# Merging VectorE's passes of a state-space scan, its inputs one state ahead and its outputs one state behind, over two pairs of PSUM banks

## The chip, the cores and the metric

One core of a Trainium2 chip runs the kernel. The metric is device time in microseconds, the median of several runs. Engines are TensorE (PE; PEld is its weight load), VectorE (DVE), ScalarE (ACT), GpSimd (POOL) and SyncE (SP), which issues the DMAs. Everything is float32; PSUM has eight banks of 128 partitions x 512 float32.

## The reference, cut to what matters

Two layers, each an "attention" and a feed-forward part with a residual and a layer norm, on 4 sequences of 1024 tokens x 256 channels. The first is a gated recurrence (gate, below). The second is a selective state-space model with 16 states per channel, and this is the part that the change touches:

```
dA[t,d,n] = exp(dt[t,d] * A[d,n])
h[t,d,n]  = dA[t,d,n] * h[t-1,d,n] + dt[t,d] * x[t,d] * B[t,n]
y[t,d]    = sum over n of h[t,d,n] * C[t,n]
```

B and C are rows of a small projection of x: one value per token and state, the same for all channels.

## The kernel before, in words

**Chunks and steps.** The tokens are cut into 8 chunks of 512, two to a sequence. Channels lie on partitions, in two halves h = 0, 1 of 128, so one state of one chunk is two tiles of 128 x 512. A written-out pipeline works in steps; in each step five chunks are in work at five stages: *ahead* (load, convolution), *gate* (the gated recurrence, norm, first feed-forward up), *prep* (feed-forward down, in-projection, convolution, B, C and dt), *scan* (the 16 states) and *tail* (out-projection, second feed-forward, store). Each engine has its own `step` function, in which the calls stand in an order written by hand; each engine runs its list in that order, and semaphores tie them. Steps 3 to 7 have all or nearly all stages; scans run from 179 to 1036 us.

**One state n of a scan.** TensorE spreads row B(n) over all partitions into one bank (`spread_B`, one matmul of 97 x 512, L1188) and C(n) into another (`spread_C`). VectorE runs `state_input` (u * B, in two passes of 128 x 512, L876), `state_scan` (the recurrence, two scans of 128 x 512, L889) and `state_output` (h * C, two passes of 128 x 512, L902). ScalarE makes dA two tiles ahead or so (`state_decay`, L594), GpSimd adds hC into y (`sum_states`, L334, 128 x 1024) and in the first chunk of a sequence saves the last column (`save_carry`). The three banks `pBC` rotate over B and C: B(n) waits for the first scan of state n-1, C(n) for the second.

**Around it on VectorE.** Between the states stand the calls of the other stages: `add_ffn0`, `readout` (y * gate, L908, needs all 15 sums), `row_stats` and `row_moments` of the norms, `log_A`, `scaled_input`, `recurrence` (L832, two scans), `mconv_silu` (L852), `x_proj_low`, `dt_x` (L863).

**TensorE's list, in part.** down(0) last half, B(1), C(1), ..., `out_proj1` before B(3), two x2 transposes before B(4), `out_proj0` (16 matmuls, needs `recurrence`) before B(8), `x_proj` (needs `mconv_silu`) and a `down` of 16 matmuls before B(10), x1 transposes (need the norm of the gate stage) after B(12), eight `up` groups, then `down` groups of 16 matmuls with B(0) of the next chunk between them.

**GpSimd's and ScalarE's lists, in part.** GpSimd: `sum_states(1)`, then `row_scales` of the prep norm. ScalarE: `normalize` of prep, `gate_tanh(1,0)`, copy of x2's first transpose, `a_squared`, the second copy and `gate_tanh(1,1)`. At the end of a step: `step_sizes` (Softplus, makes dt), then the last two relus of the feed-forward, which the first `down` waits for.

**Banks.** `pA` (2) serves gate, up and x1 transposes, `pM` (1) x2 transposes, in-projection x, x_proj and dt, `pC` (2) the token-major results, `pBC` (3) B and C.

Of the kernel before, what the change touches and what calls it, by code (L numbers as in the profile page):

```python
# [1 line left out]

# [23 lines left out]
ACT = mybir.ActivationFunctionType  # L26
# [23 lines left out]
BRING = 3  # L50
# [11 lines left out]
NCHUNK = NSEQ * PER_SEQ  # L62
LAGS = LAG_AHEAD, LAG_GATE, LAG_PREP, LAG_SCAN, LAG_TAIL = -1, 0, 1, 2, 3


def build(nc, xT, x, par, ffb, rows, gateT, outT, inT, xpT, opT, w1a, w2a, w1b, w2b, out):
    ctx = ExitStack()
    with ctx:
# [85 lines left out]
        def C_bank(n):  # L154
            return pBC[(2 * n + 1) % BRING]

        def input_banks(n):

            return pBC[(2 * n - 1) % BRING], B_bank(n)

# [8 lines left out]
            B_mm C_mm dA_ready dBx_ready h_ready carry_saved hC_ready y_sum yg_ready eps_ready x3_seeded xtok_loaded passed  # L169
# [20 lines left out]
        def apart(eng):  # L190


            eng.sem_inc(S["passed"], 1)

        def num(ch):
            return PER_SEQ * ch[0] + ch[1]

        def first(ch):

            return isinstance(ch[0], int) and num(ch) == 0  # L200


        @block.sync
        def _(sp):
# [3 lines left out]

            def load(ch):
                q, p = ch  # L210
                c = num(ch)
                if not (isinstance(q, int) and c < 2):
                    sp.wait_ge(S["tap_ready"], H * PAD * (c - 1))
                sp.dma_start(xt[p][:], xT[:, :, bass.ds(q, 1), p * T:p * T + PAD + T].rearrange("k h o t -> k h (o t)")).then_inc(xt_loaded[p], 16)

            def load_rows(ch):
                q, p = ch
                if not first(ch):
                    sp.wait_ge(sum_ready[LN_GATE], num(ch))
                sp.dma_start(xtok[:], x[:, bass.ds(q, 1), p, :, :].rearrange("k o b d -> k (o b) d")).then_inc(S["xtok_loaded"], 16)  # L220
# [17 lines left out]
            def step(ahead, gate, prep, scan, tail):  # L238

                if ahead is not None:  # L240
                    load(ahead)
                    if first(ahead):
                        load_weights()
                if gate is not None:
                    load_rows(gate)
                if tail is not None:
                    q, p = tail
                    sp.wait_ge(norm_ready[LN_OUT], TB * (num(tail) + 1))
                    sp.dma_start(out[:, bass.ds(q, 1), p, :, :].rearrange("k o b d -> k (o b) d"), x3b[:]).then_inc(S["stored"], 16)
# [6 lines left out]
        def _(pool):  # L256
# [13 lines left out]
            def row_scales(n, ch):  # L270

                c = num(ch)
                pool.wait_ge(meanvar[n], TB * (c + 1))
                nc.gpsimd.tensor_tensor(ve[n][:], mv[n][:, :, 1], eps_rows[:, 0, :], ALU.add).then_inc(ve_ready[n], 1)  # L274
                nc.gpsimd.tensor_scalar(neg_mean[n][:], mv[n][:, :, 0], -1.0, None, ALU.mult).then_inc(neg_ready[n], 1)
                pool.wait_ge(ve_ready[n], c + 1)
                nc.gpsimd.tensor_tensor(rstd[n][:], ve[n][:], minus_half[:], ALU.pow).then_inc(rstd_ready[n], 1)  # L277
                pool.wait_ge(neg_ready[n], c + 1)
                pool.wait_ge(rstd_ready[n], c + 1)
                nc.gpsimd.tensor_tensor(shift[n][:], neg_mean[n][:], rstd[n][:], ALU.mult).then_inc(shift_ready[n], 1)  # L280

            def add_bias(n, layer, src, dst, done, ch):
                pool.wait_ge(norm_ready[n], TB * (num(ch) + 1))
                if n == LN_Y and not first(ch):
                    pool.wait_ge(S["stored"], 16 * num(ch))
                b2 = rows_sb[:, 1 + layer, :].unsqueeze(1).to_broadcast([P, TB, D])
                nc.gpsimd.tensor_tensor(dst[:], src[:], b2, ALU.add).then_inc(done, 1)

            def conv_add(ch, k):

                done = PAD * num(ch) + k - 1
                if k == 1:
                    pool.wait_ge(S["conv_first"], H * (num(ch) + 1))
# [3 lines left out]
                nc.gpsimd.tensor_tensor(conv[:], conv[:], tap[:], ALU.add).then_inc(S["conv_sum"], 1)  # L297

            def mconv_add(ch, k):

                done = PAD * num(ch) + k - 1
                if k == 1:
                    pool.wait_ge(S["mconv_first"], H * (num(ch) + 1))
# [3 lines left out]
                nc.gpsimd.tensor_tensor(cv[:], cv[:], v[:], ALU.add).then_inc(S["mconv_sum"], 1)  # L307

            def inv_rms(ch):
                c = num(ch)  # L310
                pool.wait_ge(S["sq_sum"], TB * (c + 1))
                nc.gpsimd.tensor_tensor(ms[:], ssq[:], eps_rows[:, 1, :], ALU.add).then_inc(S["ms_ready"], 1)
                pool.wait_ge(S["ms_ready"], c + 1)
                nc.gpsimd.tensor_tensor(rms[:], ms[:], minus_half[:], ALU.pow).then_inc(S["rms_ready"], 1)

            def rms_residual(ch):
                c = num(ch)
                pool.wait_ge(S["o_scaled"], TB * (c + 1))
                norm_w = rows_sb[:, 0, :].unsqueeze(1).to_broadcast([P, TB, D])
                nc.gpsimd.tensor_tensor(x1[:], x1[:], norm_w, ALU.mult).then_inc(S["o_weighed"], 1)  # L320
# [1084 lines left out]
```

## Time and profile before

| what | us |
|---|---|
| median of 3 runs (lowest, highest) | 1095.97 (1095.84, 1096.62) |
| the profiled execution: time, span | 1098.24, 1096.0 |
| VectorE busy in the span | 857.7 |
| TensorE busy in the span | 819.7 |
| ScalarE, GpSimd busy | 607.3, 581.6 |
| mean granted TensorE clock | 0.871 |

The span is first to last instruction. A duration in the profile runs from an instruction's start to its end, and two neighbours on an engine can overlap, so the distance between starts (the pitch) is what an instruction costs its engine.

### The profile page before, as it was taken

To read this page: it belongs to the slowest core of one execution; us is meant where nothing else is said; L and a number is where in the kernel's file an instruction comes from. 1 tells how busy PE (TensorE), PEld (TensorE's weight loads), DVE (VectorE), ACT (ScalarE), POOL (GpSimd) and SP (SyncE) were. 2 spreads that over 40 slices of the span, in tenths; PEclk is the share of its full clock that TensorE was granted. 3 is DMA by queue.
4 is the path that set the end of the run, shared out by engine and by line. 5 is a ranking of instruction groups with operands and counts; after the bars stand their busy time and mean duration, and the time that the engine had idled before them with its cause. 6 is when DMAs were issued, how large, how long until landed. Compare 5 with 4: busy or idle time off the path is not lost. (4 is left out here: it accounts for less than half of the span.)

```text
span 1096.0 us, 8799 instructions
## 1 busy us (share of the span) xinstructions
PE 819.7 (75%) x2536; PEld 500.2 (46%) x2536; DVE 857.7 (78%) x1226; ACT 607.3 (55%) x983; POOL 581.6 (53%) x419
## 2 busy tenths in 40 slices
PE   1358559736976997799869988899779889269376
PEld 0226226323643654465526563557346646145244
DVE  0302314999799999999999999998999899999811
ACT  3533545754666676667575767565853574534221
POOL 2041251567556864778285838683656474654410
PEclk9769769866988999899898998899889989569678
DMA  8000000000000010001000010001000000000000
GB/s 306 0 19 20 0 20 19 1 0 19 1 0 1 1 58 1 0 1 59 0 1 0 1 58 0 1 1 39 1 0 1 20 1 1 19 0 1 19 0 20
DMA packets 9215, 19.43 MB, mean 18 GB/s; under 512 B 1360, under 2 KB 3920, under 8 KB 9168
## 3 DMA queue, kind: packets, MB, share of 16 engines
q1 hardware_dynamic: 9168, 18.88, 5.0%
q8 instruction: 20, 0.33, 0.1%
q14 instruction: 27, 0.22, 0.1%
HBM read 14.68 MB, written 4.19 MB: 17 GB/s over the span
## 5 line engine op out<-in xcount | busy, mean ns | idle before, releaser
L334 POOL TENSOR_TENSOR y<-y,hC 128x1024 f32<-128x1024 f32 x112 | 285.7, 2551 | 57.4 <-DVE hC L902 54.1
L1075 PE MATMUL pC<-w,hT 128*128 128x256 f32 x1024 | 234.7, 384 | 16.1 <-ACT hT L532 16.0
L594 ACT ACTIVATE dA<-dt,A_neg 128x512 f32<-128x512 f32 x256 | 174.7, 719 | 122.4 <-DVE hs L889 122.2
L1188 PE MATMUL pBC<-stack,sel 97*128 97x512 f32 x256 | 158.1, 636 | 95.5 <-DVE hs L889 94.9
L1075 PEld LDWEIGHTS pC<-w,hT 128*128 128x128 f32 x1024 | 195.9, 192 | 52.9 <-issue 18.6
L876 DVE TENSOR_TENSOR pBC<-u,pBC 128x512 f32<-128x512 f32 x256 | 164.6, 687 | 43.6 <-PE pBC L1188 42.4
L902 DVE TENSOR_TENSOR hC<-hs,pBC 128x512 f32<-128x512 f32 x256 | 160.9, 669 | 1.5 <-PE pBC L1188 1.5
L889 DVE TENSOR_TENSOR_SCAN hs<-dA,carry,pBC 128x512 f32<-128x512 f32 x128 | 156.2, 1261 | 0.0
L889 DVE TENSOR_TENSOR_SCAN hs<-dA,pBC 128x512 f32<-128x512 f32 x128 | 148.5, 1200 | 0.0
L532 ACT ACTIVATE hT<-pA,ffb_sb 128x512 f32<-128x512 f32 x128 | 86.4, 687 | 101.6 <-PE pA L1068 101.4
L1188 PEld LDWEIGHTS pBC<-stack,sel 97*128 97x128 f32 x256 | 52.8, 206 | 163.4 <-DVE hs L889 138.9
L1068 PE MATMUL pA<-x1T,w 128*128 128x512 f32 x256 | 121.8, 624 | 1.4 <-ACT x1T L524 1.4
L1068 PE MATMUL pA<-tg,w 128*128 128x512 f32 x256 | 122.1, 613 | 0.7 <-ACT tg L524 0.7
L1075 PE MATMUL pC<-out_w,st 128*128 128x256 f32 x128 | 48.9, 565 | 57.4 <-DVE st L832 57.4
L510 ACT ACTIVATE x<-x,shift,rstd 128x256 f32<-128x256 f32 x96 | 49.8, 589 | 74.5 <-POOL shift L280 74.5
L297 POOL TENSOR_TENSOR conv<-conv,yg 128x1024 f32<-128x1024 f32 x24 | 58.0, 2418 | 55.4 <-ACT yg L453 55.4
L1068 PEld LDWEIGHTS pA<-x1T,w 128*128 128x128 f32 x256 | 51.3, 201 | 59.7 <-issue 57.5
L307 POOL TENSOR_TENSOR yg<-yg,v 128x1024 f32<-128x1024 f32 x24 | 59.9, 2497 | 33.7 <-ACT v L559 33.7
L1068 PEld LDWEIGHTS pA<-tg,w 128*128 128x128 f32 x256 | 51.0, 200 | 54.9 <-issue 51.5
L1068 PE MATMUL pA<-conv,gate_w 128*128 128x512 f32 x128 | 58.8, 606 | 22.1 <-POOL conv L297 22.1
L274 POOL TENSOR_TENSOR ve<-mv,eps_rows 128x4 f32<-128x4 f32 x32 | 6.5, 202 | 128.8 <-DVE mv L772 128.8
L342 POOL COPY carry<-hs 128x2 f32<-128x2 f32 x64 | 20.4, 319 | 97.2 <-DVE hs L889 97.2
(106 smaller groups left out, 1084.1 us busy)
## 6 DMA issues: line engine op xcount, KB each, us to landing
xt<-xT SPq DMA_DIRECT2D x8, 515.0 KB, 4.9
xtok<-x SPq DMA_DIRECT2D x8, 512.0 KB, 4.7
out<-x3b SPq DMA_DIRECT2D x8, 512.0 KB, 2.8
w<-w1a SPq DMA_DIRECT2D x1, 1024.0 KB, 9.5
w<-w2a SPq DMA_DIRECT2D x1, 1024.0 KB, 11.3
w<-w1b SPq DMA_DIRECT2D x1, 1024.0 KB, 8.2
w<-w2b SPq DMA_DIRECT2D x1, 1024.0 KB, 9.9
gate_w<-gateT SPq DMA_DIRECT2D x1, 512.0 KB, 7.5
```

Source lines behind the costliest of these rows:

```text
L297: nc.gpsimd.tensor_tensor(conv[:], conv[:], tap[:], ALU.add).then_inc(S["conv_sum"], 1)
L307: nc.gpsimd.tensor_tensor(cv[:], cv[:], v[:], ALU.add).then_inc(S["mconv_sum"], 1)
L334: nc.gpsimd.tensor_tensor(y[:], so_far, hC[:, n % CRING, :, :], ALU.add).then_inc(S["y_sum"], 1)
L510: nc.scalar.activation(rows[:, b, :], rows[:, b, :], ACT.Identity, bias=shift[n][:, b:b + 1], scale=rstd[n][:, b:b + 1]).then_inc(norm_rea ...
L532: nc.scalar.activation(hT[:, f, :], pA[f % 2][:], ACT.Relu, bias=ffb_sb[:, layer, f:f + 1]).then_inc(done, 1)
L594: nc.scalar.activation(dA[:, k % ARING, :], dt[:, h, :], ACT.Exp, scale=A_neg[:, h, n:n + 1]).then_inc(S["dA_ready"], 1)
L876: V.tensor_tensor(input_banks(n)[h][:], u[ch[1]][:, h, :], B_bank(n)[:], ALU.mult).then_inc(S["dBx_ready"], 1)
L889: V.tensor_tensor_scan(hs[:, n % HRING, h, :], dA[:, k % ARING, :], input_banks(n)[h][:], 0.0 if p == 0 else carry[:, n, h:h + 1], ALU.mul ...
L902: V.tensor_tensor(hC[:, n % CRING, h, :], hs[:, n % HRING, h, :], C_bank(n)[:], ALU.mult).then_inc(S["hC_ready"], 1)
L1068: mm = nc.tensor.matmul(dst, w[:, k, lo:lo + dst.shape[0]], src(k), start=k == 0, stop=k == H - 1)
L1075: mm = nc.tensor.matmul(dst[:, b * D:b * D + D], src(k, t0), w[:, k, :], start=k == 0, stop=k == nk - 1)
L1188: return nc.tensor.matmul(dst[:], sel[0:NXK, row:row + 1].to_broadcast([NXK, P]), stack[ch[1]][0:NXK, :], start=True, stop=True)
```

## The change

The four sets of roles are rearranged:

- `pM` is gone. A tensor `pS` of four banks holds two pairs; state n uses pair n mod 2. C(n) is spread into the bank of half 0, B(n) into that of half 1. x2 transposes, in-projection x, x_proj and dt use `pA`, with new waits.
- `state_input` and `state_output` are one pass of 128 x 1024 each, with B or C broadcast over the halves.
- On VectorE input(n+1) stands right behind the scans of state n, output(n) between the two scans of state n+1. What stood around the states stands now between input(n+1) and the scans of n+1. Output 15 and sum 15 run in the next step.
- B(n) waits for the second scan of state n-2, C(n) for the first scan of state n. TensorE calls C(n-1) where it called C(n); `dt_row` moves from before the second `down` of the tail to the end of the step.
- ScalarE: `gate_tanh(1,1)` stands before the second x2 copy, `step_sizes` behind the last relu.
- Chunks become objects with a length of their own, which stays 512; the `passed` increments go.

```diff
-        pM = bank("pM")
-        pBC = [bank(f"pBC{n}") for n in range(BRING)]
+        pS = ctx.enter_context(nc.psum_tensor("pS", [P, 2, H, T], F32))
+        def inputs(n):
+            return pS[:, n % 2, :, :]
+        def C_bank(n):
+            return pS[:, n % 2, 0, :]
         def B_bank(n):
-            return pBC[2 * n % BRING]
+            return pS[:, n % 2, 1, :]
...
             def state_input(ch, n):
-                for h in range(H):
-                    V.tensor_tensor(input_banks(n)[h][:], u[ch[1]][:, h, :], B_bank(n)[:], ALU.mult)...
+                if NS * c + n >= 2:
+                    dve.wait_ge(S["hC_ready"], NS * c + n - 1)
+                V.tensor_tensor(inputs(n)[:, :, 0:ch.T], u[ch.side][:, :, 0:ch.T],
+                                B_bank(n)[:, 0:ch.T].unsqueeze(1).to_broadcast([P, H, ch.T]), ALU.mult)...
...
             def state_output(ch, n):
+                dve.wait_ge(S["h_ready"], UNITS * c + H * n + H)
+                V.tensor_tensor(hC[:, n % CRING, :, 0:ch.T], hs[:, n % HRING, :, 0:ch.T],
+                                C_bank(n)[:, 0:ch.T].unsqueeze(1).to_broadcast([P, H, ch.T]), ALU.mult)...
...
             def spread_B(ch, n):
-                    pe.wait_ge(S["h_ready"], UNITS * c + H * (n - 1) + (1 if n else H))
+                if NS * c + n >= 2:
+                    pe.wait_ge(S["h_ready"], UNITS * c + H * (n - 1))
             def spread_C(ch, n):
-                    pe.wait_ge(S["h_ready"], UNITS * c + H * n)
+                pe.wait_ge(S["h_ready"], UNITS * ch.i + H * n + 1)
             def x2_transpose(ch, h, gate):
+                if gate is not None:
+                    pe.wait_ge(S["gate_tanh"], 4 * gate.i + h + 3)
             def x_proj(ch, tail):
+                if tail is not None:
+                    pe.wait_ge(S["relu1"], FB * tail.i + FB - 1)
             def dt_row(ch, gate):
+                if gate is not None:
+                    pe.wait_ge(S["relu0"], FB * gate.i + FB - 1)
...
             def step(ahead, gate, prep, scan, tail):      
+                    state_scan(scan, 1, 1)
+                    state_input(scan, 2)
+                    add_ffn0(prep, 1, tail)
+                    row_stats(LN_PREP, prep, x2[prep.side])
+                    readout(tail, gate)
+                    row_moments(LN_PREP, prep)
+                    state_scan(scan, 2, 0)
+                    state_output(scan, 1)
+                    state_scan(scan, 2, 1)
+                    state_input(scan, 3)
...
+                    scaled_input(gate)
+                    z_silu(prep, 1)
+                    recurrence(gate)
+                    state_scan(scan, 7, 0)
+                    state_output(scan, 6)
+                    state_scan(scan, 7, 1)
+                    state_input(scan, 8)
+                    state_scan(scan, 8, 0)
+                    state_output(scan, 7)
+                    state_scan(scan, 8, 1)
+                    state_input(scan, 9)
+                    mconv_silu(prep)
+                    state_scan(scan, 9, 0)
+                    state_output(scan, 8)
+                    state_scan(scan, 9, 1)
+                    state_input(scan, 10)
+                    x_proj_low(prep)
+                    row_stats(LN_GATE, gate, x1)
+                    state_scan(scan, 10, 0)
+                    state_output(scan, 9)
+                    state_scan(scan, 10, 1)
+                    state_input(scan, 11)
+                    row_moments(LN_GATE, gate)
```

## Rows read from the trace of the kernel before

**Rows 1.** The page's first part: each engine's busy time, share of the span, instructions.

```profile
PE 819.7 (75%) x2536; PEld 500.2 (46%) x2536; DVE 857.7 (78%) x1226; ACT 607.3 (55%) x983; POOL 581.6 (53%) x419
```

**Rows 2.** Waits of VectorE from 174 to 1037: total us, times, longest.

```profile
DVE pBC L876 <- PE pBC L1188: 42.4, 24, 4.0
```

**Rows 3.** Windows: stretch, its length, busy time per engine, granted TensorE clock, DMA.

```profile
576.06:582.13 6.07, 6.07 (x16) 4.93 (x17) 4.57 (x6) 0.84 (x4) 0.00 (x0) 0.54 0.00 0
590.63:593.90 3.27, 3.27 (x18) 2.88 (x16) 3.24 (x5) 3.27 (x6) 3.19 (x3) 1.00 0.00 0
509.90:515.00 5.10, 5.10 (x17) 4.21 (x17) 3.40 (x3) 5.07 (x9) 5.10 (x3) 0.67 0.27 95
522.99:637.93 114.94, 98.11 (x319) 60.94 (x318) 109.90 (x152) 74.53 (x122) 72.61 (x44) 0.93 0.04 14
```

**Rows 4.** The page's groups of instructions: the two passes that are merged.

```profile
L876 DVE TENSOR_TENSOR pBC<-u,pBC 128x512 f32<-128x512 f32 x256 | 164.6, 687 | 43.6 <-PE pBC L1188 42.4
L902 DVE TENSOR_TENSOR hC<-hs,pBC 128x512 f32<-128x512 f32 x256 | 160.9, 669 | 1.5 <-PE pBC L1188 1.5
```

**Rows 5.** Timeline of VectorE: start, length, line, tile, count, idle before and releaser.

```profile
522.99 1.29 DVE L876 TENSOR_TENSOR pBC<-u,pBC 128x512 f32<-128x512 f32 x2 [1.87 <-PE pBC L1188]
...
528.33 1.22 DVE L908 SCALAR_TENSOR_TENSOR yg<-y,zz 128x1024 f32<-128x1024 f32 x1
529.47 1.29 DVE L876 TENSOR_TENSOR pBC<-u,pBC 128x512 f32<-128x512 f32 x2
...
575.84 1.26 DVE L876 TENSOR_TENSOR pBC<-u,pBC 128x512 f32<-128x512 f32 x2
...
582.83 1.29 DVE L876 TENSOR_TENSOR pBC<-u,pBC 128x512 f32<-128x512 f32 x2 [2.20 <-PE pBC L1188]
...
587.57 1.22 DVE L852 SCALAR_TENSOR_TENSOR v<-v,yg 128x1024 f32<-128x1024 f32 x1
...
595.71 1.29 DVE L876 TENSOR_TENSOR pBC<-u,pBC 128x512 f32<-128x512 f32 x2
596.91 2.45 DVE L889 TENSOR_TENSOR_SCAN hs<-dA,carry,pBC 128x512 f32<-128x512 f32 x2
599.28 0.35 DVE L772 BATCH_NORM_AGGREGATE mv<-st 128x2 f32<-128x6 f32 x4
...
604.87 1.26 DVE L902 TENSOR_TENSOR hC<-hs,pBC 128x512 f32<-128x512 f32 x2
606.16 1.29 DVE L876 TENSOR_TENSOR pBC<-u,pBC 128x512 f32<-128x512 f32 x2
607.37 2.44 DVE L889 TENSOR_TENSOR_SCAN hs<-dA,carry,pBC 128x512 f32<-128x512 f32 x2
...
637.93 1.29 DVE L876 TENSOR_TENSOR pBC<-u,pBC 128x512 f32<-128x512 f32 x2 [0.73 <-PE pBC L1188]
```

**Rows 6.** Timeline of TensorE in the same step.

```profile
576.06 6.42 PE L1075 MATMUL pC<-out_w,st 128*128 128x256 f32 x16 [5.94 <-DVE st L832]
...
588.84 1.96 PE L1068 MATMUL pM<-v,xp_w 128*97 128x512 f32 x4 [0.27 <-DVE v L852]
...
593.90 0.81 PE L1188 MATMUL pBC<-stack,sel 97*128 97x512 f32 x2
...
604.17 1.04 PE L1086 MATMUL pA<-ident,x 128*128 128x128 f32 x8
...
626.52 3.69 PE L1075 MATMUL pC<-w,hT 128*128 128x256 f32 x16 [2.19 <-ACT hT L532]
```

**Rows 7.** Timeline of ScalarE in the same step.

```profile
536.53 2.08 ACT L510 ACTIVATE x<-x,shift,rstd 128x256 f32<-128x256 f32 x4
...
541.73 0.69 ACT L462 ACTIVATE tg<-pA,half_bias 128x512 f32<-128x512 f32 x1
```

**Rows 8.** Timeline of GpSimd in the same step.

```profile
529.63 2.37 POOL L334 TENSOR_TENSOR y<-hC 128x1024 f32<-128x1024 f32 x1 [11.64 <-DVE yg L908]
534.76 0.20 POOL L274 TENSOR_TENSOR ve<-mv,eps_rows 128x4 f32<-128x4 f32 x1 [2.77 <-DVE mv L772]
```

More of the change, by code:

```diff
@@ L184, in chunk @@
             def chunk(i):
-                return (i // PER_SEQ, i % PER_SEQ) if 0 <= i < NCHUNK else None
+                return CHUNKS[i] if 0 <= i < NCHUNK else None
             for i in range(LAG_AHEAD, NCHUNK + LAG_TAIL):
                 step(*(chunk(i - lag) for lag in LAGS))
[L190 to L200, printed above, removed]
         @block.sync
@@ L282, in add_bias @@
             def add_bias(n, layer, src, dst, done, ch):
[L283 to L287, printed above, removed]
+                pool.wait_ge(norm_ready[n], BLOCKS[ch.i + 1])
+                if n == LN_Y and ch.i > 0:
+                    pool.wait_ge(S["stored"], 16 * ch.i)
@@ L415, in step @@
                     conv_add(ahead, 3)
-                if scan is not None:
-                    sum_states(scan, 15)
             steps(pool, step)
@@ L933, in step @@
                 if scan is not None:
[L934 to L935 removed]
+                    state_scan(scan, 0, 0)
+                if tail is not None:
+                    state_output(tail, 15)
+                if scan is not None:
+                    state_scan(scan, 0, 1)
+                    state_input(scan, 1)
                 if prep is not None:
@@ L1139, in down @@
                 weight(ch, f"w2_{layer}")
-                pe.wait_ge(relu, FB * num(ch) + FB)
+                if layer == 0 and tail is not None:
+                    pe.wait_ge(sum_ready[LN_OUT], PAIRS[tail.i + 1])
+                if layer == 1 and gate is not None:
+                    pe.wait_ge(S["o_scaled"], BLOCKS[gate.i + 1])
+                elif layer == 1 and prep is not None:
+                    pe.wait_ge(S["zz_ready"], H * (prep.i + 1))
+                pe.wait_ge(relu, FB * ch.i + FB)
@@ L1349, in step @@
                 if scan is not None:
-                    spread_C(scan, 15)
+                    spread_C(scan, 14)
+                if prep is not None:
+                    dt_row(prep, gate)
                 if gate is not None:
-                    banks_for_down0(tail)
-                    down(0, gate, 0, 0)
+                    down(0, gate, 0, 0, tail=tail)
                 if prep is not None:
@@ L1357, in step @@
                     down(0, gate, 0, 1)
-                if prep is not None:
-                    spread_C(prep, 0)
+                if scan is not None:
+                    spread_C(scan, 15)
             steps(pe, step)
```

696 lines of the change are left out of this document (351 added, 345 removed).

## Prediction

> **What bounds the kernel now.** I read the engines' busy times first: VectorE 857.7 us and TensorE 819.7 us of a span of 1096.0 [rows 1]. Before the first scan at 179 us and after the last at 1036 us VectorE has little to do, so between them it is nearly full. Its waits there come next: 42.4 us before `state_input`, 24 times, for TensorE's spread of B [rows 2]. That is the first thing that the change could return. Then one full step, from the start of input(1) at 522.99 to the next at 637.93 [rows 5]: 114.94 us, of which TensorE is busy 98.1 at a granted clock of 0.93 [rows 3]. So TensorE has a sixth of the step free, and whoever moves VectorE's needs earlier against TensorE's list finds it late. The timelines say where they meet. VectorE idles 2.20 us before input(8) (TensorE is in `out_proj0`, which `recurrence` releases), and twice about 2 us where the steps join. TensorE idles before `out_proj0`, and from the x1 transposes at 604.17 to the `down` at 626.52 it works through [rows 5, 6].
>
> **The merge.** The rows give 687 and 669 ns for one pass [rows 4], two of each per state, but their spans overlap. What a pass costs is the pitch: from 606.16 to 607.37 is 1.21 us for both input passes, from 604.87 to 606.16 is 1.29 for both outputs, 0.1 of it latency because input(12) waits for the output just before (from 595.71 to 596.91, with no such wait behind it, is 1.20). The nearest row for 128 x 1024 without contention is `readout`: 528.33 to 529.47, 1.14 us [rows 5]. So a merge gives 0.06 on the input and about 0.04 on the output: 0.1 x 128 states = 13 us on VectorE. The 0.1 latency stays, now between input(n+1) and its first scan. Bounds: the merged pass reads a broadcast and writes PSUM, which no row shows in one pass; 1.14 (readout) below, 1.21 (as two) above, so 0 to 13 us. I take 1.14. VectorE's own work in that step falls from 110.1 (114.94 less 4.9 of stalls) to 108.5.
>
> The Trainium skill (VectorE: DVE Perf Modes, on the TRN2 errata) says that a large tile pays a fixed cost once which small tiles pay each; its formula for an fp32 add has 151 cycles, an estimate of 157 ns for each of 256 passes dropped, 40 us. The trace disagrees where passes follow each other: the pitch shows 0.04 to 0.06 us.
>
> **The waits of B.** B(n) may now run a state earlier. That helps where TensorE waited, and not where TensorE was late. But VectorE now wants B(n+1) ahead of output(n), and in three places something else between hardly shrinks. I follow the step of rows 5 to 8, with t = 0 at the start of input(1). VectorE's pieces: input 1.14, output 1.14, scan 1.2.
>
> *Out-projection.* Order is input(1), add_ffn0, scan, output(0), scan, input(2), add, stats, readout: it ends at t = 9.55. `out_proj1` takes 3.3 (as the 16 matmuls whose stretch is 3.27 [rows 3]), B(3) 0.6: ready at 13.65; VectorE wants it at 13.4. Stall 0.25.
>
> *The prep norm.* `row_moments` now stands before output(1), yet GpSimd's `sum_states(1)` stands before `row_scales`. Before, sum(1) began at 529.63, 5 us ahead of row_scales at 534.76 [rows 8]. Now output(1) ends at 12.2, sum(1) at 14.65 (2.37), and ScalarE's `normalize` begins 1.8 later (534.76 to 536.53 [rows 7, 8]), at 16.45. From there to gate_tanh(1,1) is 5.2 [rows 7]; with the first transpose behind gate_tanh(1,0) I take 5.35, so it ends at 22.45. The second transpose, which now needs that tanh's bank, and B(4) take 1.2: 23.65. VectorE wants B(4) at 21.85 (C(2) is late on the same path). Stall 1.8; before none.
>
> *Recurrence.* End of `recurrence` (575.84) to input(8) (582.83) is 7.0 with `out_proj0` between [rows 5, 6]. VectorE filled this with input, two scans and output (4.8); now input(7) is already done and it has 3.6. Stall 3.35 instead of 2.2. B(9), behind three up groups, is 0.45 late.
>
> *x_proj.* `x_proj` starts at 588.84, when `mconv_silu` ends; a `down` follows, B(10) starts at 593.90 [rows 5, 6]. With 0.6 for B: 5.7. Before, input(9) to x_proj_low and stats filled 6.9 (588.79 to 595.71). Now scan, output, scan: 3.55. Stall 2.15; before none.
>
> *Last stretch.* From the second scan of state 10 (599.28) TensorE sets the pace. x1's transposes came 4.9 later, 4.55 after row_moments [rows 5, 6]. Now input(11) stands before row_moments: 6.05 after the scan. TensorE then needs 22.35 to the first `down` (604.17 to 626.52), less 1.5 of the 2.19 that it waited for the last relu, which no longer stands behind Softplus, and 11.4 to input(1) (626.52 to 637.93). Sum 38.3; VectorE's own work there is 32.6: stall 5.7. ScalarE's dA for state 0, behind Softplus, a tap and a norm, comes within 0.2 of the same point.
>
> Stalls: 0.25 + 1.8 + 3.35 + 0.45 + 2.15 + 5.7 = 13.7, against 4.9. The step takes 108.5 + 13.7 = 122.2, 7.2 more. The same count gives +8 for the third step, +5.4 to +7 for the other full ones: 34 us over five. The first scan step (no tail) gets +3.8, mostly the prep norm. The last two get +5.5: x_proj +1.6 there, out_proj1 +2.5 in the last, where it runs at low clock and readout is moved to its front, the rest in output 15's move. Sum 43.
>
> **Clock.** After 5.94 us of idling TensorE's 16 matmuls of `out_proj0` took 6.07 us at granted clock 0.54 (near its lower level, 1.2 GHz), those of a `down` 3.27 at 1.00 (2.4 GHz), and one at 0.67 5.10 [rows 3, 6]. In the new order TensorE idles some 4 us before the x1 transposes, since it can run B(12) earlier but not them, right ahead of the stretch in which it sets the pace. A bound below is 0, above 2.8 per step (the two levels of rows 3); I take 1.5 in five steps, 8 us.
>
> The Trainium skill (TensorE: Matmul & The Clock Gate, part 1) says that idling gates the array to half rate until activity returns; the trace agrees at 576.06. By it the x1 stretch would start slow in every full step: 14 us for the 8, and 1153 in all.
>
> **Other parts.** Sum 15 and output 15 in the next step: `readout` wants y 8 us after input(1), sum 15 ends about 1 us after it, hidden. Dropping `passed` and the narrower slices of full length: nothing, they are no timed work. DMAs are the same. The `pA` waits of `up(1)` and gate_mm: their tiles are free some us before, hidden by the relu chain; if not, a few tenths. `dt_row` moves behind relu 6: dt is ready at 29.5 after the scan of state 10, wanted at 28.9, inside the stall counted. The lists of SP and GpSimd are moved past nothing, but for sum 15.
>
> Forecast: 1096.0 + 43 + 8 = 1147 us of span. The profiled run's time is 1098.24, the median of runs 1095.97, so the median is taken as the span.
>
> **Rivals.**
>
> (a) *VectorE is the bound and the waits go.* For it: TensorE has 16.8 us a step free, and B may run a state ahead. Then 42.4 + 13 go: 1041 us. It decides if TensorE is always a state ahead; against it stand `out_proj0` and `x_proj`, which hang on VectorE's results just before. A weaker form keeps those and loses only half the gain, 1070.
>
> (b) *Only the two fixed chains cost* (recurrence +1.15, x_proj +2.15 in six steps, +20), the rest is made good by relaxed waits and the merge (-10): 1106.
>
> (c) *TensorE slows further*: idling in three places a step, 2.8 us at each of two: +28 on the forecast's 43, 1167 or somewhat more.
>
> (d) *Merging saves the fixed cost in full*: two passes of 687 ns and two of 669 become two of 1216 to 1220 (readout's 1.22), so 0.28 us less busy in each of 128 states, 36 us, and all of it leaves the span: 1060. The overlap of neighbours in rows 5 speaks against it. The page on VectorE named above would have it so (an estimate of 40 us by its figure).
>
> **How the numbers follow.** Forecast and its near surroundings (1125 to 1165) 0.52; (b) 0.20; (c) 0.13; (a) 0.12; (d) 0.03. From 1100 to 1172 holds (b), the forecast and nearly all of (c): 0.8 or a little more. The forecast's own range is 1125 to 1165. A measurement of this kernel tells 0.2%, 2.2 us, from nothing. Faster: (a), (d) and a sliver of (b), 0.16; same 0.03; slower 0.81.
>
> **What would show it.** Rightness: busy VectorE falls by some 35 us (spans) while its waits before the merged input grow from 42 to about 100; in a full step waits of about 1.8 before input(4) or output(2), 3.3 before input(8), 2.1 before input(10), and a row of them from input(13) to input(1), TensorE without a gap there; x2's first transpose some 19 us after input(1) rather than 15.7; full steps of about 122. It is wrong if those waits are under 1 us, if input(10) is not held by x_proj's `down`, or if merged passes have a pitch far from 1.14.

## The result, and the profile after

| | before | after |
|---|---|---|
| median (lowest, highest), us | 1096.15 (1095.84, 1096.62) | 1154.88 (1152.17, 1158.47) |
| ratio to before, 95% interval | | 1.0537 (1.0501 to 1.0574) |
| profiled execution: time, span, us | 1098.24, 1096.0 | 1152.43, 1150.6 |
| mean granted TensorE clock | 0.871 | 0.857 |

Four runs of each. Those of the kernel after lie 6.3 us apart, so a difference to its median is known to some 3 us. The change costs 58.7 us on the medians, 54.6 on the spans of the two profiled executions.

The page's first part after, to be held against [rows 1]:

```profile
PE 828.8 (72%) x2536; PEld 509.5 (44%) x2536; DVE 839.4 (73%) x970; ACT 608.0 (53%) x983; POOL 558.2 (49%) x419
```

VectorE has 256 instructions fewer and is busy 18 us less, yet the span grew. The page's groups for the two merged passes [rows 4]:

```profile
L893 DVE TENSOR_TENSOR pS<-u,pS 128x1024 f32<-128x1024 f32 x128 | 155.7, 1217 | 90.5 <-PE pS L1220 90.0
L919 DVE TENSOR_TENSOR hC<-hs,pS 128x1024 f32<-128x1024 f32 x128 | 153.0, 1195 | 8.9 <-PE pS L1220 8.8
```

And VectorE's waits over the whole span (total, times, longest):

```profile
DVE pS L893 <- PE pS L1220: 90.0, 52, 5.4
...
DVE hs L908 <- ACT dA L609: 10.0, 11, 1.4
DVE hC L919 <- PE pS L1220: 8.8, 7, 3.6
```

The wait of `state_input` for TensorE's B went from 42.4 [rows 2] to 90.0 us, the wait of `state_output` for C from 1.5 [rows 4] to 8.8, and the scans wait for ScalarE's dA, which they did not before. I went from here to the steps. From input(1) of one chunk to input(1) of the next, in us (the eighth to the end of the last output):

| step | 1 | 2 | 3 | 4 | 5 | 6 | 7 | 8 |
|---|---|---|---|---|---|---|---|---|
| before | 110.4 | 113.8 | 112.5 | 114.9 | 113.6 | 115.0 | 89.8 | 80.1 |
| after | 114.1 | 120.9 | 122.2 | 122.4 | 123.3 | 122.4 | 98.4 | 82.7 |
| more | 3.7 | 7.2 | 9.7 | 7.5 | 9.7 | 7.4 | 8.6 | 2.6 |

So nothing single happened: every step pays. The eight sum to 56.4 us; outside them the kernel after is 1.8 us shorter. Over the eight, VectorE's waits (every idle stretch above 0.15 us) grew from 39.2 to 111.7 us. The rest of the stretch, counted from start to start, is VectorE's own work, and it fell from 810.4 to 793.6. Step 4, the one of [rows 5 to 8], now runs from 542.53 to 664.98. Its window, and two of its stretches:

```profile
542.53:664.98 122.45, 101.66 (x319) 63.18 (x318) 106.52 (x122) 74.67 (x122) 69.06 (x44) 0.90 0.04 13
611.47:614.18 2.71, 2.71 (x5) 1.00 (x6) 2.71 (x3) 0.00 (x0) 2.71 (x2) 0.65 0.00 0
631.36:637.00 5.64, 5.64 (x23) 4.76 (x24) 4.70 (x4) 4.49 (x8) 5.21 (x4) 0.70 0.01 3
```

VectorE's busy time fell from 109.9 [rows 3] to 106.5, TensorE's rose from 98.1 to 101.7 for the same 319 matmuls, at a granted clock of 0.90 instead of 0.93. VectorE's timeline, with the rows that begin and end the step and its main waits:

```profile
542.53 1.21 DVE L893 TENSOR_TENSOR pS<-u,pS 128x1024 f32<-128x1024 f32 x1
543.64 0.68 DVE L793 TENSOR_TENSOR x<-pC,x1b 128x512 f32<-128x512 f32 x1
...
556.09 1.23 DVE L893 TENSOR_TENSOR pS<-u,pS 128x1024 f32<-128x1024 f32 x1 [0.37 <-PE pS L1220]
...
562.45 1.22 DVE L919 TENSOR_TENSOR hC<-hs,pS 128x1024 f32<-128x1024 f32 x1 [0.52 <-PE pS L1220]
...
566.55 1.23 DVE L893 TENSOR_TENSOR pS<-u,pS 128x1024 f32<-128x1024 f32 x1 [1.69 <-PE pS L1220]
...
603.07 1.23 DVE L893 TENSOR_TENSOR pS<-u,pS 128x1024 f32<-128x1024 f32 x1 [3.63 <-PE pS L1220]
...
618.88 1.23 DVE L893 TENSOR_TENSOR pS<-u,pS 128x1024 f32<-128x1024 f32 x1 [4.06 <-PE pS L1220]
...
633.18 1.28 DVE L908 TENSOR_TENSOR_SCAN hs<-dA,carry,pS 128x512 f32<-128x512 f32 x1 [0.71 <-ACT dA L609]
...
638.14 1.23 DVE L893 TENSOR_TENSOR pS<-u,pS 128x1024 f32<-128x1024 f32 x1 [1.38 <-PE pS L1220]
...
661.54 1.22 DVE L908 TENSOR_TENSOR_SCAN hs<-dA,pS 128x512 f32<-128x512 f32 x1 [0.97 <-ACT dA L609]
...
664.98 1.23 DVE L893 TENSOR_TENSOR pS<-u,pS 128x1024 f32<-128x1024 f32 x1
```

The waits in brackets are of input(3), output(2), input(4), input(8), input(10), scan(12), input(13) and scan(0). With input(9) 0.71, input(14) 0.72, input(15) 0.63 and `dt_x` 0.23 they sum to 15.6 us. The merged input has a pitch of 1.11 us (542.53 to 543.64). TensorE's timeline says what each wait is for:

```profile
552.02 3.72 PE L1099 MATMUL pC<-op_w,yg 128*128 128x256 f32 x16 [2.08 <-DVE yg L926]
...
561.55 0.63 PE L1110 MATMUL pA<-ident,x 128*128 128x128 f32 x4 [2.13 <-ACT tg L477]
...
564.93 1.09 PE L1110 MATMUL pA<-ident,x 128*128 128x128 f32 x4 [2.52 <-ACT tg L477]
...
596.10 6.62 PE L1099 MATMUL pC<-out_w,st 128*128 128x256 f32 x16 [3.49 <-DVE st L849]
...
611.47 2.91 PE L1092 MATMUL pA<-v,xp_w 128*97 128x512 f32 x4 [2.66 <-DVE v L870]
614.18 4.37 PE L1099 MATMUL pC<-w,hT 128*128 128x256 f32 x16
...
631.36 1.07 PE L1110 MATMUL pA<-ident,x 128*128 128x128 f32 x8 [3.53 <-ACT x L525]
...
632.49 5.30 PE L1099 MATMUL pC<-w,hT 128*128 128x256 f32 x16
...
653.57 3.69 PE L1099 MATMUL pC<-w,hT 128*128 128x256 f32 x16 [0.41 <-ACT hT L547]
```

Six times TensorE stands still, for the readout, the prep norm and the tanh behind it (two transposes), the recurrence, the convolution and the gate's norm, with a spread that VectorE needs next *behind* the matmuls it stands at. Against [rows 6], `x_proj` takes 2.91 instead of 1.96, and two groups of 16 matmuls 4.37 and 5.30 where 3.62 is usual. That is the lower clock: 0.65 and 0.70 in the two short windows above, and 0.81 from 614.18 to 618.19, where the 4.37 us lie. GpSimd's timeline shows the start of the norm's chain, `sum_states(1)` ahead of the row scales [rows 8]:

```profile
554.67 2.36 POOL L350 TENSOR_TENSOR y<-hC 128x1024 f32<-128x1024 f32 x1 [10.80 <-DVE hC L919]
556.99 0.20 POOL L290 TENSOR_TENSOR ve<-mv,eps_rows 128x4 f32<-128x4 f32 x1
```

### The profile page after: what moved, and what is told of

Same layout as the page of the kernel before. It is cut to its first block and busy times, and to the rows that moved or that the text cites. A ratio compares the mean times of both kernels' runs of the same rounds, so it can differ in the third digit from the quotient of the medians.

```text
span 1150.6 us, 8402 instructions
## 1 busy us (share of the span) xinstructions
PE 828.8 (72%) x2536; PEld 509.5 (44%) x2536; DVE 839.4 (73%) x970; ACT 608.0 (53%) x983; POOL 558.2 (49%) x419
## 3 DMA queue, kind: packets, MB, share of 16 engines
HBM read 14.68 MB, written 4.19 MB: 16 GB/s over the span
## 5 line engine op out<-in xcount | busy, mean ns | idle before, releaser
L350 POOL TENSOR_TENSOR y<-y,hC 128x1024 f32<-128x1024 f32 x112 | 264.2, 2359 | 184.0 <-DVE hC L919 181.5
L1099 PE MATMUL pC<-w,hT 128*128 128x256 f32 x1024 | 242.2, 392 | 4.8 <-ACT hT L547 4.8
L609 ACT ACTIVATE dA<-dt,A_neg 128x512 f32<-128x512 f32 x256 | 174.0, 718 | 120.9 <-DVE hs L908 120.8
L893 DVE TENSOR_TENSOR pS<-u,pS 128x1024 f32<-128x1024 f32 x128 | 155.7, 1217 | 90.5 <-PE pS L1220 90.0
L1220 PE MATMUL pS<-stack,sel 97*128 97x512 f32 x256 | 153.8, 630 | 79.3 <-DVE hs L908 79.2
L908 DVE TENSOR_TENSOR_SCAN hs<-dA,carry,pS 128x512 f32<-128x512 f32 x128 | 162.6, 1270 | 6.3 <-ACT dA L609 4.2
L908 DVE TENSOR_TENSOR_SCAN hs<-dA,pS 128x512 f32<-128x512 f32 x128 | 154.8, 1210 | 8.5 <-ACT dA L609 5.8
L919 DVE TENSOR_TENSOR hC<-hs,pS 128x1024 f32<-128x1024 f32 x128 | 153.0, 1195 | 8.9 <-PE pS L1220 8.8
L547 ACT ACTIVATE hT<-pA,ffb_sb 128x512 f32<-128x512 f32 x128 | 86.7, 684 | 108.3 <-PE pA L1092 108.2
L1220 PEld LDWEIGHTS pS<-stack,sel 97*128 97x128 f32 x256 | 52.7, 209 | 129.2 <-DVE hs L908 106.7
L1110 PE MATMUL pA<-ident,x 128*128 128x128 f32 x128 | 27.4, 368 | 84.9 <-ACT x L525 48.7
L1099 PEld LDWEIGHTS pC<-out_w,st 128*128 128x128 f32 x128 | 36.2, 291 | 67.9 <-issue 60.0
```

The lines of the kernel that those rows point to most:

```text
L350: nc.gpsimd.tensor_tensor(y[:, :, 0:ch.T], so_far, hC[:, n % CRING, :, 0:ch.T], ALU.add).then_inc(S["y_sum"], 1)
L547: nc.scalar.activation(hT[:, f, 0:ch.T], pA[f % 2][:, 0:ch.T], ACT.Relu, bias=ffb_sb[:, layer, f:f + 1]).then_inc(done, 1)
L609: nc.scalar.activation(dA[:, k % ARING, 0:ch.T], dt[:, h, 0:ch.T], ACT.Exp, scale=A_neg[:, h, n:n + 1]).then_inc(S["dA_ready"], 1)
L893: V.tensor_tensor(inputs(n)[:, :, 0:ch.T], u[ch.side][:, :, 0:ch.T], B_bank(n)[:, 0:ch.T].unsqueeze(1).to_broadcast([P, H, ch.T]), ALU.mul ...
L908: V.tensor_tensor_scan(hs[:, n % HRING, h, 0:ch.T], dA[:, k % ARING, 0:ch.T], inputs(n)[:, h, 0:ch.T], 0.0 if ch.opens else carry[:, n, h: ...
L919: V.tensor_tensor(hC[:, n % CRING, :, 0:ch.T], hs[:, n % HRING, :, 0:ch.T], C_bank(n)[:, 0:ch.T].unsqueeze(1).to_broadcast([P, H, ch.T]), ...
```

## The experiments

Theory: VectorE now asks for B a state earlier, and TensorE's list, which kept its order, has it behind fixed chains. Then moving the calls in the lists gives the time back and the merge is innocent. Rivals: the merged passes themselves cost; VectorE's work bounds the step and a removed wait comes back as the next; the clock of TensorE is the main loss. Before ran beside each group of kernels, at medians of 1096.06 to 1096.94 us. Ratios are to it, with 95% intervals; "less" and "more" are to the median of the kernel after, unless another is named.

**The merge undone, the order kept.**

```diff
-                V.tensor_tensor(inputs(n)[:, :, 0:ch.T], u[ch.side][:, :, 0:ch.T],
-                                B_bank(n)[:, 0:ch.T].unsqueeze(1).to_broadcast([P, H, ch.T]), ALU.mult)...
+                for h in range(H):
+                    V.tensor_tensor(inputs(n)[:, h, 0:ch.T], u[ch.side][:, h, 0:ch.T], B_bank(n)[:, 0:ch.T], ALU.mult)...
...
-                V.tensor_tensor(hC[:, n % CRING, :, 0:ch.T], hs[:, n % HRING, :, 0:ch.T],
-                                C_bank(n)[:, 0:ch.T].unsqueeze(1).to_broadcast([P, H, ch.T]), ALU.mult)...
+                for h in range(H):
+                    V.tensor_tensor(hC[:, n % CRING, h, 0:ch.T], hs[:, n % HRING, h, 0:ch.T], C_bank(n)[:, 0:ch.T], ALU.mult)...
```

> The changed kernel with each merged pass taken apart again into two passes of 128 x 512, at the same places and in the same banks; nothing else. By the theory of the order (time is lost where VectorE asks for B and C before the work that stands ahead of them on TensorE can be done) this is a little slower: pitch 1.20 and 1.18 us instead of 1.12 and 1.11, 0.15 us x 128 = 19 us on VectorE, of which most lies in stretches where it waits for TensorE anyway (the waits of a full step are 15 of 122 us, and the last stretch is TensorE's), so +6 to +14 over the 1154.9. By the rival (the merged pass over two banks, with a broadcast operand, is what costs) it returns a good part of the 59 us: under 1130.

Measured: 1158.03 us, 1.0556 (1.0541 to 1.0572). That is 3.2 us more than after, where 6 to 14 were expected, with intervals that overlap: in the new order the merge costs no time and brings at most a few us. VectorE's own work over the eight steps, counted as above, is 804.6 us against 793.6, so 11.0 more, but its waits are 104.7 against 111.7. The merge does save work on VectorE, and two thirds of it went into waits. The timeline of VectorE shows a state with nothing between, the input's two passes at 1.18:

```profile
1064.59 1.26 DVE L894 TENSOR_TENSOR pS<-u,pS 128x512 f32<-128x512 f32 x2
1065.77 1.27 DVE L908 TENSOR_TENSOR_SCAN hs<-dA,carry,pS 128x512 f32<-128x512 f32 x1
...
1069.33 1.26 DVE L894 TENSOR_TENSOR pS<-u,pS 128x512 f32<-128x512 f32 x2
```

And the kernel after, the same part of the last chunk:

```profile
1059.49 1.21 DVE L893 TENSOR_TENSOR pS<-u,pS 128x1024 f32<-128x1024 f32 x1
1060.78 1.28 DVE L908 TENSOR_TENSOR_SCAN hs<-dA,carry,pS 128x512 f32<-128x512 f32 x1
...
1064.28 1.21 DVE L893 TENSOR_TENSOR pS<-u,pS 128x1024 f32<-128x1024 f32 x1
```

Split, the state takes 4.74 us. Merged, it takes 4.79: the scan starts 1.29 behind the input, not 1.11, because it now needs the whole merged input just ahead of it. Where a call stands between them, this 0.18 is hidden: from 1064.28 to the next input at 1069.49 is 5.21 with a 0.60 us addition in it, 4.61 without; split, the same state takes 4.73 (1069.33 to 1074.66, less 0.60).

**Only the output merged, in the kernel before.** No order is changed; output(n) stands where it stood.

```diff
-                for h in range(H):
-                    dve.wait_ge(S["h_ready"], UNITS * c + H * n + h + 1)
-                    V.tensor_tensor(hC[:, n % CRING, h, :], hs[:, n % HRING, h, :], C_bank(n)[:], ALU.mult)...
+                dve.wait_ge(S["h_ready"], UNITS * c + H * n + H)
+                V.tensor_tensor(hC[:, n % CRING, :, :], hs[:, n % HRING, :, :],
+                                C_bank(n)[:].unsqueeze(1).to_broadcast([P, H, T]), ALU.mult)...
```

> The kernel before with only state_output merged into one pass of 128 x 1024 with C broadcast over the halves; the order, the three banks and the input passes stay. By the pitch (1.11 us for the merged output in the changed kernel, 1.18 for two in the kernel before) 0.07 us x 128 = 9 us less on VectorE, about a third of it lost where it waits for TensorE: 1087 to 1092. By the rule of a fixed cost for each pass dropped it would be 128 x 0.16 = 20 us less, 1076. If merging costs by itself it is above 1096.

Measured: 1116.08 us, 1.0171 (1.0148 to 1.0195), 19 more than before beside it. A miss in the sign. VectorE's timeline:

```profile
611.11 1.28 DVE L876 TENSOR_TENSOR pBC<-u,pBC 128x512 f32<-128x512 f32 x2
612.30 2.44 DVE L889 TENSOR_TENSOR_SCAN hs<-dA,carry,pBC 128x512 f32<-128x512 f32 x2
614.88 1.22 DVE L901 TENSOR_TENSOR hC<-hs,pBC 128x1024 f32<-128x1024 f32 x1
616.13 1.29 DVE L876 TENSOR_TENSOR pBC<-u,pBC 128x512 f32<-128x512 f32 x2
```

And the same state in before, whose output and next input stand in [rows 5]:

```profile
601.32 1.28 DVE L876 TENSOR_TENSOR pBC<-u,pBC 128x512 f32<-128x512 f32 x2
602.51 2.44 DVE L889 TENSOR_TENSOR_SCAN hs<-dA,carry,pBC 128x512 f32<-128x512 f32 x2
```

From the start of the scans to the output it is 2.58 us (612.30 to 614.88); in before it is 2.36 (602.51 to 604.87), since there the output's first pass needs only the first scan. From output to input it is 1.25 instead of 1.29. So 0.04 is gained, as in the prediction, and 0.22 lost, and the state takes 5.02 us instead of 4.84. Over the eight steps the scans cost 22.7 us more from start to start and the outputs 6.0 less: 16.7 of the 19. VectorE's other instructions took 4.7 more (`mconv_silu` alone 6.2), and its waits 3.1 less. The merged output alone loses; what lets it pay is the order of the change, which puts a scan of the next state between.

**B(10) ahead of x_proj.** The change's TensorE list, with one call moved.

```diff
+                    spread_B(scan, 10)
                     x_proj(prep, tail)
                     ...
-                    spread_B(scan, 10)
```

> The changed kernel with one call moved on TensorE: the spread of B(10) stands ahead of x_proj and the down of 16 matmuls instead of behind them. By the theory of the order the wait before input(10) (4.06 us in the full step of 542 to 665) falls to under 0.5 in each of the six steps that have it, and the time by 18 to 24 us, to 1131 to 1137. By the rival of load (TensorE has too much work at too low a clock, so a wait relieved comes back at the next B or C) the time falls by less than 8 us, and the waits before output(9), input(11) or input(13) grow by what input(10) loses.

Measured: 1122.50 us, 1.0228 (1.0210 to 1.0246): 32.4 less than after, where 18 to 24 were expected; the rival of load is out. In step 4 (116.1 us) input(10) no longer waits, and input(11) waits 0.54. Its TensorE:

```profile
597.92 1.26 PE L1220 MATMUL pS<-stack,sel 97*128 97x512 f32 x3
601.62 3.31 PE L1092 MATMUL pA<-v,xp_w 128*97 128x512 f32 x4 [2.44 <-DVE v L870]
604.76 3.62 PE L1099 MATMUL pC<-w,hT 128*128 128x256 f32 x16
```

`x_proj` is still slow, but nobody waits behind it. What exceeds the theory is clock: the 16 matmuls of `out_proj0` took 5.24 us instead of 6.62, which cut input(8)'s wait from 3.63 to 2.25, and the `down` behind the x1 transposes took 3.62 instead of 5.30, which took away input(13)'s 1.38.

**C(2) and B(4) ahead of the transposes of x2.**

```diff
+                    spread_C(scan, 2)
                     x2_transpose(prep, 0, gate)
-                    spread_C(scan, 2)
+                    spread_B(scan, 4)
                     x2_transpose(prep, 1, gate)
-                    spread_B(scan, 4)
```

> The changed kernel (1154.9) with two TensorE calls moved: C(2) ahead of x2's first transpose, B(4) ahead of its second. By the theory of the order the waits before output(2) and input(4) of 0.5 and 1.7 us go in six steps or seven, 12 to 16 us: 1139 to 1143. By the rival of load less than 5 us, as the wait turns up at the next C.

Measured: 1136.18 us, 1.0363 (1.0348 to 1.0379), 18.7 less, somewhat more than the 12 to 16 expected. The waits of output(2) and input(4) are gone from the full step (a new one of 0.84 at input(5)).

**B(8) and C(7) ahead of out_proj of half 0.**

```diff
+                    spread_B(scan, 8)
                     out_proj0(gate, prep)
-                    spread_B(scan, 8)
+                    spread_C(scan, 7)
...
-                    spread_C(scan, 7)
...
+                    spread_B(scan, 9)
...
-                    spread_B(scan, 9)
```

> The kernel after, with TensorE's spread B(8) moved ahead of out_proj of half 0, C(7) right behind it, and B(9) moved behind the fifth of the up-projection's tiles of the second half. Nothing else is moved. Theory of order (a fixed chain in TensorE's own queue makes input(8) and input(9) late): in a full step of the kernel after, input(8) waited 3.63 us and input(9) 0.71; of these 4.3 us some 3 to 4 go, out_proj moves behind the input, and x_proj and B(10) follow no earlier than their own chain allows. Six steps by 3 to 4 us: 18 to 24 us less, 1131 to 1137 us. Rival (VectorE's time is only moved to the next wait, input(10), whose 4.1 us is set by the convolution behind the recurrence and TensorE's clock): under 6 us less, 1149 to 1155.

Measured: 1125.38 us, 1.0259 (1.0244 to 1.0274): 29.5 less, more than the theory asked for, and far from the rival. A full step fell from 122.4 to 117.4: the 4.3 of input(8) and (9) are gone, input(13)'s 1.38 too, input(10) waits 3.28 instead of 4.06, and new are 1.19 at output(7) and 0.89 at scan(9). In its TensorE the later stretches run faster too:

```profile
601.17 1.96 PE L1092 MATMUL pA<-v,xp_w 128*97 128x512 f32 x4 [1.07 <-ACT hT L547]
...
619.40 1.07 PE L1110 MATMUL pA<-ident,x 128*128 128x128 f32 x8 [3.53 <-ACT x L525]
...
620.54 3.62 PE L1099 MATMUL pC<-w,hT 128*128 128x256 f32 x16
```

Its granted clock in the full step is 0.96 against 0.90, and TensorE is busy 95.7 us with the same 319 matmuls. One gap before `x_proj` less, and the `down` behind the x1 transposes takes 3.62 again.

**The gate norm's moments one place earlier on VectorE.**

```diff
                     state_scan(scan, 10, 0)
+                    row_moments(LN_GATE, gate)
                     state_output(scan, 9)
                     state_scan(scan, 10, 1)
                     state_input(scan, 11)
-                    row_moments(LN_GATE, gate)
```

> The kernel after, with the row moments of the gate's norm placed on VectorE behind scan(10) instead of behind input(11), and nothing else moved. Theory (in the last stretch TensorE paces VectorE from the second norm's transposes on, and these wait for ScalarE's normalize, which waits for the moments): the transposes start about 2.3 us earlier, waits of input(13) to input(15), 2.7 us in the full step of the kernel after, shrink by 1.5 to 2.3: over five or six steps 8 to 13 us less, 1141 to 1147 us. Rival (the moments are early enough, ScalarE's dA tiles hold the scans at states 12 and 0): within 3 us of the kernel after, 1152 to 1158.

Measured: 1125.27 us, 1.0269 (1.0251 to 1.0286): 29.6 less, where 8 to 13 were expected. Its full step (532.41 to 650.00) is 117.6, and its TensorE:

```profile
617.63 1.07 PE L1111 MATMUL pA<-ident,x 128*128 128x128 f32 x8
...
619.14 3.62 PE L1100 MATMUL pC<-w,hT 128*128 128x256 f32 x16
```

The transposes start 3.05 us after the start of the second scan of state 10, not 6.75, without an idle in front, and the `down` behind them takes 3.62, not 5.30. So 3.7 of chain and 1.7 of clock left; the waits of scan(12), input(13), (14), (15), dt_x and scan(0), 4.6 us in after, are all gone from this step. My expectation had only the chain, and too short.

**Softplus ahead of the last relu, as before.** It undoes ScalarE's move of `step_sizes` except for one relu.

```diff
-                    relu(0, gate, 7)
                     step_sizes(prep)
+                    relu(0, gate, 7)
```

> The kernel after, with ScalarE's step sizes (the Softplus of the next step) placed ahead of the last relu of the gate's feed-forward. All else as in the kernel after. It puts a piece of work of about 2.7 us ahead of the relu for which TensorE's down-projection waits. Theory (TensorE's chain sets the end of the step): the down-projection and the next B are later by 2 to 2.7 us in each of six steps, less what dA of states 0 gains: 10 to 16 us more, 1165 to 1171 us. Rival (the wait of input(0) and scan(0) for ScalarE sets the end): 3 to 6 us less, 1149 to 1152.

Measured: 1172.55 us, 1.0697 (1.0681 to 1.0713), 17.7 more, where 10 to 16 were expected. The sign is right and the rival out. ScalarE's timeline, then TensorE's:

```profile
664.88 1.28 ACT L596 ACT_TABLE_LOAD   x1
666.52 1.45 ACT L596 ACTIVATE dt<-pA,par_sb 128x512 f32<-128x512 f32 x2 [0.35 <-PE pA L1219]
667.86 0.69 ACT L547 ACTIVATE hT<-pA,ffb_sb 128x512 f32<-128x512 f32 x1
```

```profile
668.69 5.38 PE L1098 MATMUL pC<-w,hT 128*128 128x256 f32 x16 [2.21 <-ACT hT L547]
```

TensorE waits 2.21 instead of 0.41 before the `down`, and then takes 5.38 for it, not 3.69: 1.8 of chain and 1.7 of clock. Their sum, 3.5, is what step 4 grew by (125.96 us against 122.45). VectorE shows it as new waits of 2.79 at input(0), 1.05 at output(15) and 1.41 at input(1), with those of `dt_x` and scan(0) gone.

**All the places at once.** TensorE: B(3) ahead of out_proj1, C(2) and B(4) as above, B(8) and C(7) around out_proj0, B(10) ahead of x_proj. GpSimd: the row scales of the prep norm ahead of sum 1.

```diff
-                    sum_states(scan, 1)
                     row_scales(LN_PREP, prep)
+                    sum_states(scan, 1)
...
+                    spread_B(scan, 3)
                     out_proj1(tail, prep)
-                    spread_B(scan, 3)
...
```

> The changed kernel with calls moved so that no B or C stands behind the long work that it need not wait for: on TensorE B(3) ahead of out_proj1, C(2) and B(4) ahead of x2's two transposes, B(8) ahead of out_proj0 and C(7) right behind it, B(10) ahead of x_proj; on GpSimd the prep norm's row_scales ahead of sum_states(1). By the theory of the order a full step loses 0.4 + 2.2 + about 2.5 + 4 of its waits, 8 to 9 us in each of some six steps: 1100 to 1108. By the rival of load less than 20 us are returned in all: above 1135.

Measured: 1098.40 us, 1.0013 (1.0004 to 1.0022), 56.5 less than after, a little below the range expected. The order of the lists is worth nearly all of the 58.7 that the change had lost. What is left in the full step (114.8) is mainly this wait of input(9), behind `up` groups, on VectorE:

```profile
584.09 1.23 DVE L893 TENSOR_TENSOR pS<-u,pS 128x1024 f32<-128x1024 f32 x1 [3.04 <-PE pS L1220]
```

**And B(9) and the moments.** The same with B(9) behind up group 5 and the gate's moments behind the first scan of state 10.

```diff
+                    spread_B(scan, 9)
                     up(1, tail, 6)
...
-                    spread_B(scan, 9)
...
+                    row_moments(LN_GATE, gate)
...
-                    row_moments(LN_GATE, gate)
```

> The version with six TensorE calls and one GpSimd call moved (1098.4), and two more moves: on TensorE the spread of B(9) behind up group 5 of the tail instead of behind group 7; on VectorE row_moments of the gate stage behind the first scan of state 10 instead of behind input(11). By the theory of the order the wait of 3.0 us before input(9) falls under 1 in six steps, and x1's transposes and with them the last stretch, in which TensorE sets the pace, begin 1 to 2 us earlier in five: 16 to 24 us less, 1074 to 1082. By the rival of load TensorE gives it back in the last stretch: above 1090.

Measured: 1066.60 us, 0.9733 (0.9717 to 0.9748): faster than both kernels, by 29.5 than before. From the last kernel it is 31.8, where 16 to 24 were expected. Its full step, as a window, and its VectorE's wait for B:

```profile
506.61:614.77 108.16, 95.02 (x319) 60.59 (x318) 105.62 (x121) 74.45 (x122) 68.27 (x44) 0.95 0.05 15
```

```profile
DVE pS L893 <- PE pS L1221: 12.0, 14, 2.4
```

108.2 us, of which VectorE is busy 105.6: here rival (a), VectorE at its bound, has come true in kind, though not at its 1041 us, and only with lists to match.

**dA of state 0 right behind Softplus.** On ScalarE, on top of the last kernel.

```diff
-                    state_decay(scan, 0)
...
+                    state_decay(prep, 0)
```

> The version before it (B(9) and row_moments moved) with one ScalarE call moved: dA of state 0 of the next chunk right behind step_sizes instead of behind the last convolution tap and the norm of the output. By the theory of the order, in which ScalarE is the second to hold the joint of two steps (waits for dA of 0.97 and 1.4 us there), 0.5 to 1 us in each of seven joints: 3 to 7 us less than c1. If the joint hangs on the spread of B(1) behind three down groups alone, no change within 2 us.

Measured: 1068.08 us, 0.9744 (0.9728 to 0.9761): no gain. The theory's 3 to 7 us were a miss, and the alternative, no change within 2 us, held. The joint of two steps still hangs on TensorE's B(1): at the end of step 4 scan(0)'s wait of 0.96 for dA is gone, and input(1) waits 1.41 for TensorE instead.

**And its passes split.** The edit of the first experiment on top of this one.

> The version c2 with each merged pass taken apart into two of 128 x 512 at the same place. It asks what the merge itself is worth once VectorE seldom waits for TensorE. By pitch 0.15 us x 128 = 19 us more on VectorE; since some of it still falls into waits, +10 to +19 over c2. By the rule of a fixed cost for each pass it would be +40. If the merge itself is worth nothing, within 3 us of c2.

Measured: 1073.40 us, 0.9794 (0.9780 to 0.9809), 5.3 us more than the last kernel, and less than the range expected. VectorE's own work over the eight steps is 797.0 us against 786.8, its waits 28.4 against 31.4. In kind it agrees with the two pitches above: 0.12 gained where a call stands between input and scan, 0.05 lost where none does.

This last kernel still beats before by 22.7 us, with every pass split. So of the 28.0 us that the kernel ahead of it gained on before, the merge has 5.3 and the order of the calls, with the banks that allow it, the rest. No run moved calls in the lists of before alone, so how much of the 22.7 needs the new order on VectorE is not shown.

## Why the prediction was right, by its steps

Forecast 1147 us of span, measured 1150.6 (median 1154.88): right in sign, size and cause.

**The two named chains behind the recurrence and the convolution: right, one under-sized.** Input(8) waited 3.63 for a forecast 3.35. Input(10) waited 4.06 for 2.15. From the start of `x_proj` to input(10) I had counted 5.7 at full clock; it took 7.41 (611.47 to 618.88), 1.7 more, because `x_proj` and its `down` ran at low clock behind 2.66 us of idling. The moves of B(8) and B(10) show both by experiment.

**The prep norm: right.** The first transpose came 19.0 us after input(1) (561.55), the second 22.4 (22.45 forecast); stalls 0.52 + 1.69 against 1.8. **Out-projection** 0.37 against 0.25 (the prediction's own terms, 9.55 + 3.3 + 0.6, give 13.45 and not its 13.65, so a stall of 0.05), **input(9)** 0.71 against 0.45.

**The last stretch: mechanism right, stall over-sized.** The waits there are 4.6 us, for 5.7 and 1.5 of clock. The clock term was right in place and size: 5.30 instead of 3.62 behind the x1 transposes, and the two runs in which it went, the move of the moments and that of B(8), show it. TensorE's way from the scan of state 10 to input(1) was 39.2 (625.80 to 664.98) against 38.3 + 1.5; but VectorE's own work in it was 34.5, not 32.6. Half of that is `dt_x`, 2.11 us rather than 1.22. The other half is a slip of mine: the prediction's pieces with the calls between them, as the trace of before has them, sum to about 33.6. The first `down` waited 0.41 instead of 2.19 for its relu, 1.8 for the 1.5 named; that ScalarE's move gives this back was shown by undoing it.

**The merge: right on VectorE, not in the time.** The pitch was 1.11, not 1.14. VectorE's own work in step 4 came to 122.45 - 15.6 = 106.8, against a forecast 108.5. Over the eight steps the split passes cost VectorE 11.0 and 10.2 us, near the 13 forecast, though not 0.1 for every state alike. In the time they cost 3.2 us (hardly told from nothing) and 5.3, since waits took up much of the rest. VectorE's own work fell by 16.8 us in all; what the merge did not bring came from other instructions that ran faster or slower than before, some of them beside GpSimd (last section), and the prediction did not have it. Rival (d), 1060, is out. The Trainium skill's fixed cost (VectorE: DVE Perf Modes, on the TRN2 errata), an estimate of 40 us, was not found: undoing the merge moved the time by 3.2 and 5.3 us.

**The sum by steps.** Five full steps: forecast 34 + 7.5 of clock = 41.5, measured 7.2 + 9.7 + 7.5 + 9.7 + 7.4 = 41.5. The first: 3.8 and 3.7. The last two: 5.5 forecast, 8.6 + 2.6 = 11.2 measured. This is the mis-sized term. In step 7 `out_proj1` waited 5.35 us for VectorE's readout and then took 6.75 us, against 3.72 before: the low clock that I had there only in step 8. Its input(3) waited 3.52. Input(10) waited 4.19, where before had 0.47 and I had added 1.6.

**Where luck helped.** That the five full steps agree to a tenth is partly luck. For step 4 the forecast was 108.5 + 13.7 + 1.5 = 123.7, and 106.8 + 15.6 = 122.4 were measured. Input(10) is 1.9 over and the smaller stalls together 1.1; the last stretch is 2.6 under and VectorE's own work 1.7.

**The signs named beforehand.** Waits before the merged input about 100: they were 90.0, and 8.8 at the output. Steps of about 122: 120.9 to 123.3. VectorE's busy time down by 35: it fell by 18. I had summed mean durations, 687 and 669 ns, whose overlaps the busy time counts once: the two groups' busy times, 164.6 + 160.9 before [rows 4], are 155.7 + 153.0 now, 17 less.

**The rivals.** (b), 1106, is out: it had nothing for the two norms' chains, and moving calls out of their way alone returned 18.7 and 29.6 us. (a) needs other lists, above. (c) was half true: the lower clock cost about 1.7 us at each of two places in the full step, not 1.5 at one and not 2.8 at two, and other terms were smaller.

**What stays open.** Moves taken alone gave 32.4, 18.7, 29.5 and 29.6 us, each more than expected; together with two more, B(3) and GpSimd's row scales, they gave 88.3, not 110. Some of each is TensorE's clock, which rose in other stretches too. How the parts divide was not taken further. Nor was the move of the x2 transposes to `pA`, which makes them wait for ScalarE's tanh, undone by itself; it lies within the prep norm's chain.

## What to carry to other kernels

When an engine's calls are moved a place ahead, list for each thing it asks for what stands before it in its maker's queue: here six matmul groups that hang on VectorE's own newest results, some by way of GpSimd and ScalarE, stood ahead of the small spread that VectorE wanted next, and moving nine calls turned 5% slower into 2.7% faster. A gap in TensorE can cost twice where its list paces others, once as the gap and once as matmuls at the lower clock behind it. Merge two passes only with another instruction between the merged one and whoever reads it, price it by the distance between starts, not by durations, and expect waits to take part of what it saves.

## What the runs showed of the hardware

- **The same gap, two clocks.** The x1 transposes waited 3.53 us in after and in the run with B(8) moved. The 16 matmuls behind took 5.30 us in the one and 3.62 in the other; some 20 us earlier the one had idled 2.66 us before `x_proj` and ran at a granted 0.65 behind it, while the other had idled 1.07 and took 1.96 for `x_proj`. The Trainium skill (TensorE: Matmul & The Clock Gate, part 1) has idling gate the array to half rate; the granted clock of 0.65 and 0.70 in the windows after the gaps agrees in kind. But the length of the last gap alone did not say which it would be: in the run with B(8) moved, the clock from 619.40 to 624.20, behind the same 3.53 us, is 1.00.
- **A dependent neighbour on VectorE starts late by 0.14 to 0.22 us**: scan behind merged input 1.29 instead of 1.11 (0.18), input behind merged output 1.25 instead of 1.11 (0.14); and a merged output behind the two scans whose results it needs 2.58 after their start instead of 2.36 (0.22). Half passes hide it, since each needs only one half.
- **What VectorE loses beside GpSimd moves, it doesn't vanish.** In step 4 the two scans of the recurrence together fell from 5.99 to 3.94 us: before, GpSimd was busy in 4.92 of the 5.92 us from their start to the next instruction, after in 1.69 of 3.87. But `tg<-tg,conv`, of the same shape in both, rose from 1.21 to 3.39. After, it began at 577.08, while an addition of GpSimd ran from 576.56 to 579.38. Before, it began at 560.77, 0.15 us ahead of GpSimd's sum, and there it was the sum that took 3.29 us instead of 2.36.
